# A four-layer transformer with cross attention: the softmax normalisation of the second batch moves from GpSimd to VectorE

## What is computed

```python
def attention(xn, ctx, h):                  # one of 16 heads; L1X and L3X differ in head size, mask and bias
    scores = q(xn)[h] @ k(ctx)[h].T * scale + added      # 128 x 120; added: causal and length mask, or a bias
    p = exp(scores - scores.max(-1))
    return (p / p.sum(-1)) @ v(ctx)[h]
```

## Time and profile before

| | |
|---|---|
| median of 3 runs | 759.89 us (757.17 to 760.71) |
| profiled execution | 758.24 us, of which 756.9 us from the first to the last instruction |
| TensorE busy | 680.3 us (90%) |
| VectorE busy | 495.9 us (66%) |
| ScalarE busy | 369.6 us (49%) |
| GpSimd busy | 188.8 us (25%) |
| mean granted TensorE clock | 0.937 of full speed |

### The profile page before, as it was taken

The page is one execution under the profiler, slowest core; times in us unless marked ns, Lnnn a source line. Parts: engine busy times, 40 slices in busy tenths (PEclk is TensorE's granted clock), DMA queues, the critical chain, the costliest instruction groups (busy, mean ns, idle before and its releaser), DMA issues.

```text
span 756.9 us, 14486 instructions
## 1 busy us (share of the span) xinstructions
PE 680.3 (90%) x5496; PEld 599.8 (79%) x5496; DVE 495.9 (66%) x1289; ACT 369.6 (49%) x1281; POOL 188.8 (25%) x256
## 2 busy tenths in 40 slices
PE   5759998899999898889999997999999996879887
PEld 4559996769999795759999995769999894557675
DVE  1946557948776848948767667858767477155635
ACT  2420204971363833971366535872365635636473
POOL 1000006342101606342201416423101407420130
PEclk9869998699999999899999998899999998899969
DMA  9659992039836511057833703049816400000000
GB/s 349 288 187 349 374 382 63 2 125 353 303 104 229 168 57 29 1 169 270 308 116 133 266 1 118 3 146 347 292 65 207 156 29 7 1 1 1 2 1 8
DMA packets 33189, 113.71 MB, mean 150 GB/s; under 512 B 3680, under 2 KB 7264, under 8 KB 32736
## 3 DMA queue, kind: packets, MB, share of 16 engines
q1 hardware_dynamic: 33120, 112.78, 42.3%
HBM read 111.72 MB, written 1.05 MB: 149 GB/s over the span
## 4 chain that ended last, share of the span: by engine, by line
PE 59%; DVE 18%; ACT 10%; POOL 5%; DMA 3%; issue 2%; SPq 0%; POOLq 0%; DVEq 0%
PE f_bank L459 29%; PE bank L459 26%; ACT wide_b L1103 4%; DMA gated<-gates_of 3%; DVE gated L1431 3%; PE bank L655 2%; DVE f_route L1431 1%; POOL rstd L1322 1%; DVE max_neg L1690 1%; DVE wide_b L1434 1%; DVE x L1434 1%; ACT f_b L1039 1%; ACT wide_a L988 1%; POOL wide_b L1331 1%; PE f_bank L552 1%
## 5 line engine op out<-in xcount | busy, mean ns | idle before, releaser
L459 PE MATMUL f_bank<-weights,gated 128*128 128x128 f32 x2048 | 245.2, 278 | 9.1 <-DVE gated L1431 8.8
L459 PEld LDWEIGHTS f_bank<-weights,gated 128*128 128x128 f32 x2048 | 237.0, 194 | 13.4 <-issue 11.4
L1103 ACT ACTIVATE wide_b<-wide_b,max_neg 128x120 f32<-128x120 f32 x272 | 103.6, 386 | 25.5 <-DVE max_neg L1690 19.7
L1322 POOL TENSOR_TENSOR rstd<-var_eps,w_const 128x1 f32<-128x1 f32 (+1 forms) x56 | 44.6, 796 | 253.4 <-DVE var_eps L1427 253.2
L1431 DVE TENSOR_TENSOR gated<-gated,f_b 128x1024 f32<-128x1024 f32 x64 | 81.5, 1296 | 29.0 <-ACT f_b L988 15.4
L1331 POOL TENSOR_TENSOR wide_b<-wide_b,row_inv 128x480 f32<-128x480 f32 x64 | 72.0, 1130 | 104.9 <-DVE row_inv L1695 104.7
L1431 DVE TENSOR_TENSOR gated<-gated,f_xnT 128x1024 f32<-128x1024 f32 x64 | 76.8, 1224 | 19.6 <-DMA gated<-gates_of 19.4
L988 ACT ACTIVATE wide_a<-bank 120x512 f32<-120x512 f32 (+4 forms) x109 | 57.3, 550 | 52.4 <-PE bank L655 14.4
L655 PE MATMUL bank<-w_const,wide_b 128*120 128x128 f32 x256 | 46.5, 323 | 13.2 <-POOL wide_b L1331 12.9
L1286 POOL TENSOR_TENSOR f_rstd<-f_var_eps,w_const 128x1 f32<-128x1 f32 x24 | 13.3, 559 | 175.3 <-DVE f_var_eps L1427 175.1
L1103 ACT ACTIVATION_READ_ACCUMULATOR wide_b<-wide_b,max_neg 128x1 f32 x272 | 52.2, 192 | 0.0
(11 more groups left out here) (236 smaller groups left out, 1202.2 us busy)
## 6 DMA issues: line engine op xcount, KB each, us to landing
gated<-gates_of SPq DMA_DIRECT2D x128, 512.0 KB, 6.3
weights<-in_experts SPq DMA_DIRECT2D x64, 512.0 KB, 6.8
w_L2f<-in_L2f SPq DMA_DIRECT2D x1, 2124.0 KB, 15.0
w_L3x<-in_L3x SPq DMA_DIRECT2D x1, 2108.0 KB, 19.1
wide_b<-in_raw0f SPq DMA_DIRECT2D x1, 1024.0 KB, 5.6
w_L3f<-in_L3f SPq DMA_DIRECT2D x1, 1000.0 KB, 21.8
w_L1f<-in_L1f SPq DMA_DIRECT2D x1, 516.0 KB, 9.3
x_next<-in_x SPq DMA_DIRECT2D x4, 128.0 KB, 5.9
```

The lines of the kernel that those rows point to most:

```text
L459: return nc.tensor.matmul(o, lhsT, rhs, start=first, stop=last)
L1103: last = nc.scalar.activation(p, p, ACT.Exp, bias=max_neg[lane][:, h:h + 1], accum_out=row_sum[lane][:, h:h + 1])
L1322: nc.gpsimd.tensor_tensor(rstd[lane][:, cols], var_eps[lane][:, cols], part["const", "minus_half"][:, 0:cols.stop - cols.start], ALU.pow)\
```

## The change

For lane 1 alone, GpSimd no longer issues the multiplication; its `ahead()` stays where it was, so its front steps keep their places. VectorE issues the same multiplication directly behind its own reciprocal of lane 1, waits for that reciprocal first, and counts up the same semaphore `probs_normed`. This is in both L1X and L3X, so 4 groups x 2 layers x 4 pairs = 32 instructions move. Lane 0 stays as it was.

```diff
                     def normalise_probs(layer):
                         for i in range(4):
                             for lane in LANES:
+                                if lane == 1:
+                                    ahead()
+                                    continue
                                 pool.wait_ge(inv_ready[lane], inv_ready.upto(layer, i + 1, pair))
                                 p3 = wide_b[lane][:, 4 * K * i:4 * K * (i + 1)].rearrange("p (h k) -> p h k", k=K)
                                 nc.gpsimd.tensor_tensor(
...
                         dve.wait_ge(probs_ready[lane], probs_ready.upto(layer, i + 1, pair))
                         nc.vector.reciprocal(row_inv[lane][:, 4 * i:4 * i + 4], row_sum[lane][:, 4 * i:4 * i + 4])\
                             .then_inc(inv_ready[lane], 1)
+                        if lane == 1:
+                            dve.wait_ge(inv_ready[lane], inv_ready.upto(layer, i + 1, pair))
+                            p3 = wide_b[lane][:, 4 * K * i:4 * K * (i + 1)].rearrange("p (h k) -> p h k", k=K)
+                            tt(p3, p3, row_inv[lane][:, 4 * i:4 * i + 4].unsqueeze(2).broadcast_to([128, 4, K]),
+                               ALU.mult).then_inc(probs_normed[lane], 1)
```

## The result

The changed kernel takes 762.26 us (median of 20 runs, 759.49 to 766.24); the kernel before, run beside it, 759.65 us (20 runs). The ratio is 1.0035 with a 95% interval of 1.0020 to 1.0051, that is +2.6 us (+1.5 to +3.9). I had forecast 762.6 us and a sum of +2.7. The profiled execution after the change took 760.75 us, 759.5 of it span, against 758.24 and 756.9 before: +2.5. So the total is as forecast. The stages are not all, as the rest shows.

The account below looks back on a forecast made before the run. TensorE, busy for 90% of the span, was taken to bound the kernel. Stage terms summed to +2.7 us, taking the profiled 758.24 to 760.9; with the median 1.65 above, 762.6 us was forecast, range 756.5 to 768.

Parts of the forecast that it names:

- queue price: On VectorE's queue: each moved instruction adds 0.69 us, taking 0.77 in place of 0.08; 22 us for all 32.
- the refunds in L1X of pair 1: VectorE instructions held up by GpSimd get shorter, 1.09 to 0.42 and 1.52 to 0.84 us; with idle time, 1.6 back.
- the full cover in L3X of pair 1: VectorE falls behind by up to 2.1 us, but TensorE, busy 21.00 of 21.00 us, hides it: 0.
- the tail of L3X of pair 2: Lane 0's last normalisation comes 0.7 us later, its reciprocal delayed and a `gated` product starting first: +0.7.
- L1X of pair 1, +0.8 in the sum: Three moved instructions on the chain cost 2.1 us, 1.6 comes back, the fourth meets lane 0's normalisation for 0.3.
- L1X of pair 2: Two late moved instructions cost 1.4 us, less 0.3 in the gate and 0.3 on `f_xn`: +0.8.
- L3X of the last pair, "+0.4": Lane 0's third reciprocal and its transposition come later, so lane 1's transposition starts at 727.0, not 726.53: +0.4 us.
- an L3X tail shorter by over 1 us: Sign of being wrong: the ends of the L3X stages get shorter by over 1 us.
- L1X longer by over 1.5 us each: Sign of being wrong: the windows of the L1X stages get longer by over 1.5 us each.
- The refunds come, the costs are hidden: Whole kernel: TensorE's 12.9 us wait for normalisations halves and nothing is paid; up to -6 us, 753 to 756; chance 0.1.
- VectorE becomes the bound: VectorE on or near the chain: 771 without refunds, 764 to 768 with later `gated` tiles or lock meetings; chance 0.3.
- Nothing on the chain moves: Whole kernel: TensorE's 90% busy time covers gains and costs alike, 759 to 761 us; chance 0.2.

## Why the prediction was right, and where it was not

**Right by its own steps.** The queue price (0.69 forecast, 0.70 measured), the instruction's length (0.66, median 0.658), the refunds in L1X of pair 1, the full cover in L3X of pair 1 (21.00 of 21.00 us again), and the tail of L3X of pair 2 in place, order and size. L1X as the seat of the cost was right as well: L1X alone gives +2.75 us, L3X alone nothing or a gain.

**Mis-sized: L1X of pair 1, +0.8 in the sum, +1.5 in the trace.** The mechanism was the one described, moved instructions on the chain less refunds. What the sum had no term for is the lower clock level behind TensorE's longer idle time. With L1X alone moved, and in the changed kernel with added products, the level held at that place, and the same stage cost +0.7, as forecast. In L1X of pair 2 the sum was high by 0.4. The two stages together come to 1.0 to 1.9 us in the four traces that move them for lane 1 alone, against my 1.6. The medians ask for more, +3.2 for these two stages (the interval begins at +1.8), and where the rest would lie isn't shown.

**Wrong in sign: L3X of the last pair, "+0.4".** The queue's part is real (0.2 us at the product's start, 0.4 in the stage when the clock gives nothing back). But I held TensorE's durations at the level that they had in the trace of before, for a stage whose spacing the change alters. Moving four instructions there alone gave -1.8 us, and pairing the transpositions without any move shortened the stage by 1.1 us. The prediction had named an L3X tail shorter by over 1 us as a sign of being wrong, and that sign came. (The other, L1X longer by over 1.5 us each, did not: 1.5 in pair 1, less in pair 2.) It had also said that delays of tenths can move the stretches of low clock, without a sign; that is what happened.

**So the total agreed partly by luck.** Errors of -1.6 us in L3X of the last pair and -0.4 in L1X of pair 2 stand against +0.7 in L1X of pair 1, +0.4 in L1X of the last pair, and +0.7 in the start and between stages. The start, 0.4 us, lies ahead of the first moved instruction and isn't the change's doing. That the two profiled executions differ by nearly as much as the medians is luck as well, since the start alone lies up to 4.2 us off the kernel before in the other traces.

**The rivals.** *The refunds come, the costs are hidden*: the refunds are real (with both lanes moved nearly all of the surplus is gone), but the costs are not hidden: 6.7 us by themselves. *VectorE becomes the bound*: not at 32 instructions, certainly at 64 (+14.0 us). *Nothing on the chain moves*: the interval of +1.5 to +3.9 us excludes it, and the pieces (+3.2, -3.4) show that it would only have looked so.

**Open.** Why the granted clock returns in time with paired transpositions and the product close behind, and not with single ones, with a wait before the product, or with added products, isn't settled; the runs show which instructions ran at which level, not the rule. Nor is it shown that the lower level in the stretch from 653 to 700 us was caused by the moves in L1X; two single executions with it and a lower mean clock point that way, and two executions of kernels that move all of L1X without it point the other.

## What to carry to other kernels

Price a moved instruction on the queue that receives it (its length, plus its wait, less the overlap), stage by stage, and price the refund on the same queue; take away cost and relief one at a time, since they needn't add. A change of a few tenths that alters the spacing of TensorE's work should be tried per stage rather than for all stages: here the whole move costs 2.6 us, and the same move in two of eight stages gains 3.4. Where matmuls ran at the lower clock level, don't carry their durations over as constants.

## What the runs showed of the hardware that I had not expected

- The same 16 matmuls of L3X take 1.98 or 1.09 us, and a transposition of four heads 1.11 or 0.65, by the clock level alone. Which one is met in a stage went with the spacing just ahead: upper where the transpositions came in pairs with the product directly behind, lower where they came singly, and lower too where they came in pairs and TensorE waited 1.09 us before the product.
- Work added to keep the clock up can lose it: three products of 512 columns kept the upper level for five transpositions and had the lower one some 5 us after the last of them, also in the kernel that had the upper level there without them.
- A chain of lock meetings passes on: `gated` (1.19 us) holds a normalisation on GpSimd (1.88 instead of 0.99), which holds the next product on VectorE (1.24 instead of 0.66).
